# Piece products as 128 + 64 rows, two steps' half-height products in a row, and a new end of the routed sum, in a two-layer ViT tower

## The chip, the cores and the metric

The kernel runs on one core of a Trainium2 chip. The metric is the device time of one execution in microseconds (us), lower is better. All times below are those of one core.

## The reference, cut to what matters

Activations are 1,024 tokens (64 images of 16 patches) by 192 features, in float32. After the patch embedding come four residual blocks, each behind a layer norm:

```python
h = tok(x)
h = h + attn0(layernorm(h))                 # 12 heads over the 16 patches of an image
h = h + ffn0(layernorm(h))                  # soft mixture: 4 experts x 256 slots
h = h + attn1(layernorm(h))                 # low-rank causal attention
h = h + ffn1(layernorm(h))                  # routed mixture: 4 of 32 experts for a token
# ffn0
logits = einsum('bnd,esd->bnes', x, phi)    # 1024 logits for a token
dispatch = softmax(logits, axis=1)          # over the 16 tokens of an image
combine = softmax(logits.reshape(B, N, E*S))
slots = einsum('bnd,bnes->besd', x, dispatch)
hid = gelu(einsum('besd,edh->besh', slots, w1) + b1)
y = einsum('besh,ehd->besd', hid, w2) + b2
out = einsum('besd,bnes->bnd', y, combine)
# ffn1: comb holds 4 non-zero gates for each token
h = gelu(einsum('nd,edm->nem', xf, W1) + b1)
out = einsum('ne,ned->nd', comb, einsum('nem,emd->ned', h, W2) + b2)
```

## The kernel before

Tokens stand in 8 tiles of 128. The stages follow each other, each in a block of its own in which every engine has its own instruction list, with counted semaphores between them. SP's list issues nearly all DMAs, POOL's the indirect ones; a wait in a list holds everything behind it.

**layernorm** (L150) is called ahead of each of the four blocks. DVE normalises a tile (L188), PE transposes it in two pieces of 96 features (L199), ACT copies the pieces to `xnT` (96 partitions, two chunks, 1,024 tokens; L211).

**slot_weights** (L729). For each tile PE computes 1,024 logits: two halves of 512 columns, each the sum of two products of 96 rows (L770 to L773). PE also transposes logits and weights (L764), ACT copies and exponentiates, DVE takes maxima and sums. PE's order is logits 0, logits 1, then for each tile transposes of the logits, transposes of the weights of the tile before, logits of the tile two on.

**hidden_pieces** (L876) computes x·w1 for all tokens (3,072 columns) and writes it, and the transposed dispatch weights, to DRAM (`pieces`) as three bf16 pieces that add up to the float32 value. There are 8 tiles of 5 steps. Step 0 is 8 transposes (L934). Steps 1 to 4 are one expert each: two halves of 384 columns, each the sum of two float32 products of 96 rows (L939). A float32 product is two matmul instructions in the trace, so such a step has 8 instructions. A step's result lies in one of 4 PSUM buffers (`gps`). ACT makes the first piece ("one", L961), DVE subtracts it into `rest` (L984, semaphore `rest1`), ACT makes the second piece ("two", L955), DVE the third by another subtraction (L978, semaphore `three`). ACT's order is one(n), second(n-1); DVE's is rest(n), third(n-1). PE may start step n when `rest1` says that step n-4 has left its buffer (L931). The pieces of a tile stand in one of two SBUF buffers (`gp`); from tile 2 on ACT waits until the stores of the tile two before have landed (L960). SP stores a tile in three DMAs (L903): after step 0, after step 2, after step 4. Behind the stores of tile 2 SP's list has the loads of the first two images for the next stage (L912 to L918): 3 small ones and 12 of `load_image`.

**slot_experts** (L990) runs the 64 images in sequence and is the longest stage. Its PE needs the two images and all earlier work of the block before.

**expert_tiles** (L1425) runs the routed experts: 63 tiles of 128 rows, 3 buffers deep, 9 tiles in a loop body. PE transposes gathered rows (L1496), then computes the 6 hidden chunks as full-height products of 128 rows and half-height products of 64 rows, the latter in two row groups in turn (L1508, L1511), and the result of the tile before (L1523). DVE scales it into `y` (L1598) and POOL adds it by an indirect DMA to the rows of one of three sums in DRAM (`sums`: the output and two others; L1644), one sum for each buffer. In the last round the last three tiles all go to the output, each waiting for the one before. POOL adds the third sum to the second (L1661) once both are complete, and, after the last tile, the second to the output (L1669). Each of these is a DMA with addition in DRAM (L1649). The kernel ends when the last has landed.

Of the kernel before, what the change touches and what calls it, by code (L numbers as in the profile page):

```python
# [15 lines left out]
P = 128  # L16
# [25 lines left out]
KQ = 64  # L42
# [107 lines left out]
def layernorm(nc, g, stage, banks=None, loads=(), loaded=None):  # L150
# [4 lines left out]
    with Scope(nc, stage) as s:  # L155
# [5 lines left out]
            s.sem(n) for n in ("stats_ready", "mv_ready", "step", "var_ready", "sd_ready", "xn_ready", "t_ready", "xnT_done"))  # L161
        block = s.block()

# [6 lines left out]
        def _(dve):  # L170
# [16 lines left out]
            for i in range(TILES):  # L187
                dve.tensor_scalar(g.xn[:, i, :], g.h[:, i, :], r[:, i:i + 1], nmr[:, i:i + 1],  # L188
                                  ALU.mult, ALU.add).then_inc(xn_ready, 1)

        @block.tensor
        def _(pe):
            pe.wait_ge(g.ident_in, 16)
            keep_busy(pe, g, psT[-1], 16)
            for i in range(TILES):
                pe.wait_ge(xn_ready, i + 1)
                for k in range(NKD):
                    at = (i % 2 * NKD + k) * P
                    tr = pe.transpose(psT[i // 2][0:KD, at:at + P], g.xn[:, i, k * KD:(k + 1) * KD], g.ident[:])  # L199
                tr.then_inc(t_ready, 1)  # L200

        @block.scalar
        def _(act):
            act.wait_ge(var_ready, 1)
            act.activation(sd[:], ve[:], ACT.Sqrt).then_inc(sd_ready, 1)
            for j in range(TILES // 2):
                act.wait_ge(t_ready, 2 * j + 2)
                for k in range(NKD):
                    src = psT[j][0:KD, :].rearrange("p (i k c) -> p i k c", i=2, k=NKD)[:, :, k, :]
                    dst = g.xnT[:, k, 2 * j * P:(2 * j + 2) * P].rearrange("p (i c) -> p i c", i=2)  # L210
                    act.activation(dst, src, ACT.Copy).then_inc(xnT_done, 1)  # L211
# [517 lines left out]
def slot_weights(nc, g, CT, Dn, zn):  # L729

    with Scope(nc, "slw") as s:
# [26 lines left out]
        def _(pe):  # L759
# [7 lines left out]
            def logits(i):  # L767
                if i >= 2:
                    pe.wait_ge(lg_ready, i - 1)
                for half in range(2):  # L770
                    for k in range(NKD):
                        mm = pe.matmul(cl[:, i % 2, half, :], g.xnT[:, k, i * P:(i + 1) * P],
                                       g.phi[:, k, half * 512:(half + 1) * 512], start=(k == 0), stop=(k == NKD - 1))  # L773
# [102 lines left out]
def hidden_pieces(nc, g, Dn, b1, b2_rows, pieces, b_dram):  # L876
# [3 lines left out]
    with Scope(nc, "hid") as s:  # L880
        gp = s.sb("gp", [P, 2, 3, ALL], BF16)
        rest = s.sb("rest", [P, 2, ALL_SLOTS])
# [3 lines left out]
        b_in, step, g_ready, one, rest1, two, three, b_done, g_out = (  # L886
            s.sem(n) for n in ("b_in", "step", "g_ready", "one", "rest1", "two", "three", "b_done", "g_out"))
# [4 lines left out]

        def half_of(e):
            return 512 if e == 0 else HALF

        @block.sync
        def _(sp):
# [7 lines left out]
            for i in range(TILES):  # L905
                sp.wait_ge(three, STEPS * i + 1)
                store(i, slice(WIDE, ALL))
                for half in range(2):
                    sp.wait_ge(three, STEPS * i + 2 * half + 3)
# [11 lines left out]
        def _(pool):  # L921
            for i, dT in enumerate(g.dT):
                pool.memset(dT[PROWS:BROWS, :], 1.0).then_inc(g.ones, 1)
                pool.wait_ge(g.ones, i + 1)

        @block.tensor
        def _(pe):
            pe.wait_ge(g.w1_in, 16)
            for n, (i, e) in enumerate(steps):
                if n >= 4:  # L930
                    pe.wait_ge(rest1, n - 3)  # L931
                if e == 0:
                    for c in range(SLOT_CHUNKS):
                        mm = pe.transpose(gps[n % 4][:, c // 4, (c % 4) * P:(c % 4 + 1) * P], Dn[:, c, i * P:(i + 1) * P], g.ident[:])  # L934
                else:
                    for half in range(2):
                        for k in range(NKD):
                            at = (e - 1) * HID + half * HALF
                            mm = pe.matmul(gps[n % 4][:, half, 0:HALF], g.xnT[:, k, i * P:(i + 1) * P],  # L939
                                           g.w1[:, k, at:at + HALF], start=(k == 0), stop=(k == NKD - 1))  # L940
                mm.then_inc(g_ready, 1)

        def piece(buf, k, e):
            at = slice(WIDE, ALL) if e == 0 else slice((e - 1) * HID, e * HID)
            return gp[:, buf, k, at].rearrange("p (a c) -> p a c", a=2)

        def left(n, e):
            return rest[:, n % 2, 0:2 * half_of(e)].rearrange("p (a c) -> p a c", a=2)
# [872 lines left out]
```

## Time and profile before

| | |
|---|---|
| three runs | 1148.75, 1153.36, 1153.44 us; median 1153.36 |
| the profiled execution | 1146.11 us, of which the span from its first to its last instruction is 1144.3 us |
| mean granted clock of TensorE in it | 0.946 of full speed |
| PE, matmuls | 1015.9 us busy (89%) |
| ACT | 671.7 us (59%) |
| DVE | 403.2 us (35%) |
| POOL | 232.7 us (20%) |

The stages in the profiled execution, by the times at which they start: attention 0 and what is ahead of it 0 us, the layer norm 84, slot_weights 89, hidden_pieces 148, slot_experts 246, attention 1 about 690, routing about 775, expert_tiles 823 to 1144.3.

How to read it: the profiled execution's time is 1.8 us above its span, and lies 7.2 us under the median of the three runs. Busy time of PE is modelled at the end of each matmul, so a group of matmuls shows slightly longer than the distance to the next group. A clock of 1.0 is 2.4 GHz, one of 0.5 is 1.2 GHz.

### The profile page before, as it was taken

What the parts mean: (1) busy time and instruction counts of PE and PEld (TensorE: products, weight loads), DVE (VectorE), ACT (ScalarE), POOL (GpSimd) and SP (SyncE); (2) the same over time, 40 slices, a digit from 0 to 9 for tenths busy, and PEclk for the clock granted to TensorE, in tenths of its full rate; (3) what the DMA queues carried; (4) which work ended last, traced back from release to release, by engine and by line L of the source; (5) the groups of instructions that cost most, each with busy time, mean ns of one, the idle gap of its engine ahead of it and who ended that gap; (6) DMA issues with size and microseconds to landing.
All of it is one profiled execution on the core that took longest, in us unless ns stands there. A gap on an engine that the chain in (4) does not pass through costs nothing. (4 is left out here: it accounts for less than half of the span.)

```text
span 1144.3 us, 22007 instructions
## 1 busy us (share of the span) xinstructions
PE 1015.9 (89%) x7432; PEld 668.2 (58%) x7432; DVE 403.2 (35%) x1027; ACT 671.7 (59%) x1227; POOL 232.7 (20%) x236
## 2 busy tenths in 40 slices
PE   8879689989999999999999998873299999999992
PEld 7455456633444444444445454452189999999992
DVE  2666968750111111111111115767822222222220
ACT  0657957679988888888788852451033433343330
POOL 0110310000000000000000000200655555555532
PEclk9999889989999999999999998896589999999997
DMA  9200037979555445455444401004199999999994
GB/s 278 79 2 0 1 125 262 340 270 172 120 117 134 111 114 127 95 124 124 112 111 117 106 1 46 0 6 129 49 326 313 311 307 306 309 309 307 304 288 73
DMA packets 72411, 183.74 MB, mean 161 GB/s; under 512 B 15712, under 2 KB 30400, under 8 KB 72008
## 3 DMA queue, kind: packets, MB, share of 16 engines
q1 hardware_dynamic: 59260, 166.24, 48.7%
q0 software_dynamic: 12640, 16.16, 7.1%
q8 instruction: 53, 0.87, 0.3%
q10 hardware_dynamic: 432, 0.26, 0.1%
q14 instruction: 26, 0.21, 0.1%
HBM read 147.52 MB, written 36.67 MB: 161 GB/s over the span
## 5 line engine op out<-in xcount | busy, mean ns | idle before, releaser
L1145 ACT ACTIVATE sle_H<-sle_hp 128x1024 f32<-128x1024 f32 x384 | 367.5, 1024 | 61.1 <-PE sle_hp L1082 61.1
L1565 ACT ACTIVATE ext_H<-ext_hp,ext_bias 128x128 f32<-128x128 f32 x378 | 104.3, 375 | 171.9 <-issue 153.8
L1099 PE MATMUL sle_up<-sle_H,sle_cw 128*32 128x512 f32 (+1 forms) x2048 | 193.5, 496 | 0.0
L1523 PE MATMUL ext_yp<-ext_w,ext_H 128*128 128x192 f32 x756 | 139.7, 335 | 2.2 <-ACT ext_H L1565 1.6
L1160 DVE STREAM_TRANSPOSE sle_UT<-sle_up 128x256 f32<-128x256 f32 x64 | 37.3, 583 | 295.1 <-PE sle_up L1099 295.1
L1523 PEld LDWEIGHTS ext_yp<-ext_w,ext_H 128*128 128x128 f32 x756 | 121.1, 190 | 10.0 <-issue 2.6
L1082 PE MATMUL sle_hp<-keep_G,keep_dT 99*128 99x512 bf16 (+1 forms) x512 | 103.6, 337 | 10.9 <-PEq L880 5.7
L1099 PEld LDWEIGHTS sle_up<-sle_H,sle_cw 128*32 128x32 f32 x2048 | 53.8, 109 | 87.6 <-issue 74.2
L1082 PE MATMUL sle_hp<-sle_G,sle_dT 99*128 99x512 bf16 (+1 forms) x512 | 99.9, 327 | 1.1 <-ACT sle_H L1145 1.1
L1067 POOL COPY sle_cw<-keep_CT 128x128 f32 (+1 forms) x64 | 18.7, 293 | 396.1 <-PE sle_up L1099 396.0
L1508 PE MATMUL ext_hp<-ext_xT,ext_w 128*128 128x128 f32 x756 | 96.1, 277 | 0.0
L1082 PEld LDWEIGHTS sle_hp<-keep_G,keep_dT 99*128 99x128 bf16 x512 | 45.6, 100 | 82.4 <-issue 30.0
L1508 PEld LDWEIGHTS ext_hp<-ext_xT,ext_w 128*128 128x128 f32 x756 | 90.6, 194 | 0.3 <-DMA ext_w<-W 0.3
L939 PE MATMUL hid_gps<-pre_w,vit_xnT 96*128 96x384 f32 x256 | 85.7, 494 | 0.0
L1082 PEld LDWEIGHTS sle_hp<-sle_G,sle_dT 99*128 99x128 bf16 x512 | 44.4, 98 | 69.4 <-ACT sle_H L1145 30.3
L1576 DVE COPY ext_yi<-rmoe_slot 128x1 uint32 (+1 forms) x63 | 9.7, 154 | 208.1 <-PE ext_yp L1523 172.9
L1644 POOL DMA_INDIRECT sum<-ext_y,ext_yi x40 | 63.4, 1584 | 71.0 <-DVE ext_gate L1589 32.7
L939 PEld LDWEIGHTS hid_gps<-pre_w,vit_xnT 96*128 96x128 f32 x256 | 49.0, 194 | 32.8 <-issue 1.7
L1108 PE MATMUL sle_up<-keep_w,sle_UT 128*128 128x192 f32 x384 | 67.3, 326 | 0.8 <-DVE sle_UT L1160 0.8
L1631 POOL DMA_INDIRECT ext_x<-xn,ext_xi x63 | 62.1, 985 | 27.3 <-issue 18.6
L1108 PEld LDWEIGHTS sle_up<-keep_w,sle_UT 128*128 128x128 f32 x384 | 61.7, 190 | 2.1 <-DVE sle_UT L1160 1.7
L1511 PE MATMUL ext_hp<-ext_xT,ext_w 64*128 64x128 f32 x756 | 59.7, 291 | 0.0
(258 smaller groups left out, 1158.2 us busy)
## 6 DMA issues: line engine op xcount, KB each, us to landing
ext_w<-W SPq DMA_DIRECT2D x126, 576.0 KB
pieces<-hid_gp SPq DMA_DIRECT2D x16, 1152.0 KB, 4.9
keep_G<-pieces SPq DMA_DIRECT2D x32, 288.0 KB, 3.9
sle_G<-pieces SPq DMA_DIRECT2D x32, 288.0 KB, 3.8
pieces<-hid_gp SPq DMA_DIRECT2D x8, 768.0 KB, 4.7
keep_G<-pieces SPq DMA_DIRECT2D x32, 192.0 KB, 3.8
sle_G<-pieces SPq DMA_DIRECT2D x32, 192.0 KB, 3.7
keep_CT<-xT SPq DMA_DIRECT2D x6, 512.0 KB, 6.2
```

The lines of the kernel that those rows point to most:

```text
L939: mm = pe.matmul(gps[n % 4][:, half, 0:HALF], g.xnT[:, k, i * P:(i + 1) * P], g.w1[:, k, at:at + HALF], start=(k == 0), stop=(k == NKD - 1))
L1082: mm = pe.matmul(hp[k % DEEP][:, j, off:off + width], dT[b][:, c * P:(c + 1) * P], G[b][:, (c // 2) * HID + at:(c // 2) * HID + at + width ...
L1099: mm = pe.matmul(to[32 * e:32 * e + 32], cw[:, p, 2 * e + grp, :], H[:, p, h:h + width], start=(p == 0 and grp == 0), stop=(p == 1 and grp ...
L1108: mm = pe.matmul(yps, UT[:, par, b, :], g.w2[:, b, :], start=(b == blocks[0]), stop=(b == blocks[-1]))
L1145: act.activation(H[:, p, WIDTH * k:WIDTH * (k + 1)], hp[k % DEEP][:].rearrange("p a c -> p (a c)"), ACT.Gelu_apprx_tanh).then_inc(gelu_don ...
L1160: dve.transpose(UT[:, par, at // 32:(at + width) // 32, 32 * j:32 * j + 32], src.rearrange("p (b c) -> p b c", c=32)).then_inc(ut_done[ban ...
L1508: pe.matmul(hp[q][:, c % 2, (c // 2) * P:(c // 2 + 1) * P], w1[:, q, c, :], xT[:, q, 0, :], start=(c < 2), stop=False)
L1511: mm = pe.matmul(hp[q][:, c % 2, (c // 2) * P:(c // 2 + 1) * P], w1[rows, q, HC + c // 2, :], xT[rows, q, 1, :], start=False, stop=(c >= H ...
L1523: mm = pe.matmul(yp[:, 0:D], H[:, q, c, :], w2[:, q, c, :], start=(c == 0), stop=(c == HC - 1))
L1565: act.activation(H[:, q, c, :], hp[q][:, c % 2, (c // 2) * P:(c // 2 + 1) * P], ACT.Gelu, bias=bias[:, q, c:c + 1]).then_inc(gelu_done, 1)
L1631: pool.indirect_dma_start(out=x[:, p, :], out_offset=None, in_=xn_dram, in_offset=bass.IndirectOffsetOnAxis(ap=xi[p][:], axis=0)).then_inc ...
L1644: pool.indirect_dma_start(out=sums[to], out_offset=bass.IndirectOffsetOnAxis(ap=yi[q][:], axis=0), in_=y[:, q, :], in_offset=None, compute ...
```

## The change

Four edits:

1. `layernorm` has a form `wide`, used ahead of `slot_weights`: POOL copies features 128 to 191 of each tile once more behind feature 191 (`xn` has 256 columns now), and PE transposes two full chunks of 128. Rows 0 to 127 of the first chunk are features 0 to 127; of the second, rows 0 to 63 and rows 64 to 127 both are features 128 to 191. `phi` and `w1` are laid out to match on the host, with the same number of bytes.
2. In `slot_weights` each half's logits are a product of 128 rows and one of 64 rows; the two halves' 64-row products use different row groups and stand behind each other.
3. `hidden_pieces` does the same, over two steps (experts) at a time: first the four full-height products of both, then their four half-height ones. `rest` has three buffers instead of two. The third pieces of steps 2 and 4 are made by POOL instead of DVE, with semaphores `three_dve` and `three_pool` for those who wait.
4. In `expert_tiles` the last two tiles are not scattered. DVE makes 0/1 matrices `place` from their row numbers, PE multiplies them with `y` (8 token tiles x 2), SP loads the three sums to SBUF, DVE adds them and the products in PSUM, and SP stores the result to the output in two halves. The two additions in DRAM are gone.

```diff
 def layernorm(...):
+        if wide:
+            @block.gpsimd
+            def _(pool):
+                for i in range(TILES):
+                    pool.wait_ge(xn_ready, i + 1)
+                    pool.tensor_copy(g.xn[:, i, D:D + KQ], g.xn[:, i, P:D]).then_inc(twice_ready, 1)
...
+                if wide:
+                    pe.wait_ge(twice_ready, i + 1)
+                    for k in range(NKD):
+                        tr = pe.transpose(psT[i // 2][:, at + k * P:at + (k + 1) * P], g.xn[:, i, k * P:(k + 1) * P], g.ident[:])
 def slot_weights(...):
                 for half in range(2):
-                    for k in range(NKD):
-                        mm = pe.matmul(cl[:, i % 2, half, :], g.xnT[:, k, i * P:(i + 1) * P],
-                                       g.phi[:, k, half * 512:(half + 1) * 512], start=(k == 0), stop=(k == NKD - 1))
+                    pe.matmul(cl[:, i % 2, half, :], g.wideT[:, 0, i * P:(i + 1) * P], g.phi[:, half * 512:(half + 1) * 512],
+                              start=True, stop=False)
+                for half in range(2):
+                    rows = slice(half * KQ, (half + 1) * KQ)
+                    mm = pe.matmul(cl[:, i % 2, half, :], g.wideT[rows, 1, i * P:(i + 1) * P], g.phi[rows, ALL_SLOTS:],
+                                   start=False, stop=True)
 def hidden_pieces(...):
-        rest = s.sb("rest", [P, 2, ALL_SLOTS])
+        rest = s.sb("rest", [P, 3, ALL_SLOTS])
+        ON_POOL = (2, 4)
...
         def _(pool):
+            for n, (i, e) in enumerate(steps):
+                if e in ON_POOL:
+                    pool.wait_ge(two, n + 1)
+                    pool.tensor_tensor(piece(i % 2, 2, e), left(n, e), piece(i % 2, 1, e), ALU.subtract).then_inc(three_pool, 1)
 
         @block.tensor
+            def free(n):
                 if n >= 4:
                     pe.wait_ge(rest1, n - 3)
...
+                for pair in range(1, STEPS, 2):
+                    for e in (pair, pair + 1):
+                        free(STEPS * i + e)
+                        for half in range(2):
+                            pe.matmul(gps[(STEPS * i + e) % 4][:, half, 0:HALF], g.wideT[:, 0, tokens],
+                                      g.w1[:, e - 1, half * HALF:(half + 1) * HALF], start=True, stop=False)
+                    for e in (pair, pair + 1):
+                        for half in range(2):
+                            rows = slice(half * KQ, (half + 1) * KQ)
+                            mm = pe.matmul(gps[(STEPS * i + e) % 4][:, half, 0:HALF], g.wideT[rows, 1, tokens], g.w1[rows, e - 1, HID:],
+                                           start=False, stop=True)
+                        mm.then_inc(g_ready, 1)
         @block.vector
-                if n >= 2:
-                    dve.wait_ge(three, n - 1)
+                if n >= 3:
+                    wait_thirds(dve, *steps[n - 3])
                 dve.tensor_tensor(left(n, e), gps[n % 4][:, :, 0:half_of(e)], piece(i % 2, 0, e), ALU.subtract).then_inc(rest1, 1)
-                if n >= 1:
+                if n >= 1 and steps[n - 1][1] not in ON_POOL:
                     third(n - 1)
 def expert_tiles(...):
         @block.sync
             program(sp, load)
+            sp.wait_ge(y_out[1], 16 * (MOE_TILES // DEEP - 1))
+            sp.dma_start(second[:], by_lane(sums[1])).then_inc(second_in, 16)
+            sp.wait_ge(first_out, 32)
+            sp.wait_ge(y_out[0], 16 * (MOE_TILES // DEEP))
+            sp.dma_start(g.h[:], by_lane(out)).then_inc(first_in, 16)
+            sp.wait_ge(y_out[2], 16 * (MOE_TILES // DEEP - 1))
+            sp.dma_start(third[:], by_lane(sums[2])).then_inc(third_in, 16)
+            for j in range(2):
+                half = slice(j * TILES // 2, (j + 1) * TILES // 2)
+                sp.wait_ge(whole, 2 * j + 2)
+                sp.dma_start(by_lane(out)[:, half], second[:, half]).then_inc(total_out, 16)
         @block.tensor
             down(MOE_TILES - 1, BODY - 1, ROUNDS - 1)
+            pe.wait_ge(place_ready, PLACED)
+            pe.wait_ge(y_done, MOE_TILES)
+            for i in range(TILES):
+                for n in range(PLACED):
+                    mm = pe.matmul(hp[i // 4][:, i % 4 // 2, i % 2 * D:(i % 2 + 1) * D], place[:, n, i, :], y[:, (n - PLACED) % DEEP, :],
+                                   start=(n == 0), stop=(n == PLACED - 1))
+                if i % 2 == 1:
+                    mm.then_inc(placed, 1)
         @block.vector
+            def total():
+                dve.wait_ge(second_in, 16)
+                dve.wait_ge(first_in, 16)
+                c.after(dve.tensor_tensor(second[:], second[:], g.h[:], ALU.add))
+                dve.wait_ge(third_in, 16)
+                c.after(dve.tensor_tensor(second[:], second[:], third[:], ALU.add))
+                for j in range(4):
+                    pair = second[:, 2 * j:2 * j + 2]
+                    dve.wait_ge(placed, j + 1)
+                    dve.tensor_tensor(pair, pair, hp[j // 2][:, j % 2, 0:2 * D].rearrange("p (a d) -> p a d", a=2), ALU.add).then_inc(whole, 1)
         @block.gpsimd
-            merge(0, 1)
-            pool.wait_ge(merged, 32)
+            pool.wait_ge(y_out[0], 16 * (MOE_TILES // DEEP))
```

Besides, SP loads two small constants (68 KB) behind the first store of the output in `expert_tiles`, and DVE makes the two `place` matrices in the last round, at tiles 55 and 57.

## Rows read from the trace of the kernel before

**Rows 1.** Busy time by stage: us, PE, PEld, DVE, ACT, POOL, clock, DMA share, GB/s

```profile
89.00:148.00 59.00, 45.27 (x194) 27.40 (x195) 45.56 (x64) 48.53 (x98) 15.74 (x9) 0.90 0.00 1
148.00:241.00 93.00, 92.17 (x320) 56.60 (x319) 74.94 (x81) 63.16 (x79) 1.60 (x2) 0.97 0.72 266
```

**Rows 2.** Timeline of PE in hidden_pieces: start us, us, engine, line, operation

```profile
147.75 1.94 PE L934 MATMUL hid_gps<-vit_ident,pre_Dn 128*128 128x128 f32 x8 [3.21 <-PEq L732]
...
184.02 1.04 PE L934 MATMUL hid_gps<-vit_ident,pre_Dn 128*128 128x128 f32 x8
184.89 10.49 PE L939 MATMUL hid_gps<-pre_w,vit_xnT 96*128 96x384 f32 x32
195.22 1.04 PE L934 MATMUL hid_gps<-vit_ident,pre_Dn 128*128 128x128 f32 x8
```

**Rows 3.** The chain that ended last, one routed tile: start us, us, what

```profile
1103.40 1.34 PE ext_hp L1508 x12
1104.74 0.87 PE ext_hp L1511 x12
1105.61 2.15 PE ext_yp L1523 x12
```

**Rows 4.** Timeline at the end of hidden_pieces, ACT, DVE and PE

```profile
240.21 0.81 ACT L961 ACTIVATE hid_gp<-hid_gps 128x768 bf16<-128x768 f32 x1 [0.70 <-PE hid_gps L939]
...
242.40 1.95 DVE L978 TENSOR_TENSOR hid_gp<-hid_rest,hid_gp 128x768 bf16<-128x768 f32 x2
...
245.87 4.42 PE L1082 MATMUL sle_hp<-keep_G,keep_dT 99*128 99x512 bf16 x13 [5.70 <-PEq L880]
```

**Rows 5.** Groups of instructions, each shape apart, POOL: busy us, mean ns

```profile
L860 POOL TENSOR_TENSOR pre_Dn<-pre_Dn,slw_dsum 128x1024 f32<-128x1024 f32 x8 | 15.4, 1931 | 51.3 <-DVE slw_dsum L832 51.3
L1067 POOL COPY sle_cw<-keep_CT 128x128 f32<-128x128 f32 x16 | 4.6, 292 | 83.1 <-PE sle_up L1099 83.0
```

**Rows 6.** Timeline in routing, POOL and DVE side by side

```profile
806.15 1.46 POOL L1288 TENSOR_TENSOR rte_row_in<-rte_in_tile,rte_row_lane 128x504 bf16<-128x504 f32 x1
806.65 2.05 DVE L1404 TENSOR_TENSOR rte_in_lane<-rte_lane,rte_lanef 128x1024 bf16<-128x1024 f32 x1
```

**Rows 7.** Timeline of SP's DMA issues and of ACT in hidden_pieces

```profile
189.10 0.53 SPq L903 DMA_DIRECT2D pieces<-hid_gp  x1
...
201.01 2.60 SPq L903 DMA_DIRECT2D pieces<-hid_gp  x2
...
211.54 1.02 ACT L961 ACTIVATE hid_gp<-hid_gps 128x1024 bf16<-128x1024 f32 x1 [3.38 <-DMA pieces<-hid_gp]
```

**Rows 8.** Busy time of three short stretches, columns as in rows 1

```profile
203.00:205.00 2.00, 2.00 (x8) 1.20 (x7) 1.51 (x3) 0.97 (x2) 0.00 (x0) 1.00 1.05 404
250.00:252.00 2.00, 2.00 (x8) 0.97 (x7) 0.00 (x0) 2.00 (x3) 1.88 (x4) 0.50 0.19 57
1129.00:1131.00 2.00, 0.00 (x0) 0.00 (x0) 0.00 (x0) 0.00 (x0) 1.50 (x1) 0.59 0.00 0
```

**Rows 9.** Timeline at the start of slot_weights, DVE

```profile
97.55 1.22 DVE L842 TENSOR_REDUCE slw_dmax<-slw_dl 128x64 f32<-128x1024 f32 x1 [2.03 <-PE slw_dl L764]
```

**Rows 10.** Timeline of the end of the kernel

```profile
1118.21 1.55 POOL L1644 DMA_INDIRECT out<-ext_y,ext_yi  x1 [3.05 <-DVE ext_y L1598]
...
1124.44 0.41 DVE L1598 TENSOR_SCALAR ext_y<-ext_yp,ext_gate 128x192 f32<-128x192 f32 x1
...
1133.00 0.96 POOL L1649 DMA_DIRECT2D out<-sum  x1 [2.50 <-DMA out<-ext_y,ext_yi]
```

**Rows 11.** The chain that ended last, its DMAs at the end

```profile
1122.85 5.21 DMA out<-ext_y,ext_yi
1128.93 3.52 DMA out<-ext_y,ext_yi
```

**Rows 12.** DMA issues by line: count, KB each, median us from issue to landing

```profile
pieces<-hid_gp SPq DMA_DIRECT2D x16, 1152.0 KB, 4.9
xn<-vit_xn SPq DMA_DIRECT2D x1, 768.0 KB, 4.2
out<-sum POOLq DMA_DIRECT2D x1, 768.0 KB, 7.0
```

More of the change, by code:

```diff
@@ L147, in _, with layernorm @@
             dve.wait_ge(h_done, TILES)
-def layernorm(nc, g, stage, banks=None, loads=(), loaded=None):
+def layernorm(nc, g, stage, banks=None, loads=(), loaded=None, wide=False):
     with Scope(nc, stage) as s:
@@ L928, in _ @@
             pe.wait_ge(g.w1_in, 16)
-            for n, (i, e) in enumerate(steps):
+            def free(n):
                 if n >= 4:
                     pe.wait_ge(rest1, n - 3)
[L932 to L948, printed above, removed]
+            for i in range(TILES):
+                tokens = slice(i * P, (i + 1) * P)
+                free(STEPS * i)
+                for c in range(SLOT_CHUNKS):
+                    tr = pe.transpose(gps[STEPS * i % 4][:, c // 4, (c % 4) * P:(c % 4 + 1) * P], Dn[:, c, tokens], g.ident[:])
+                tr.then_inc(g_ready, 1)
+                for pair in range(1, STEPS, 2):
[10 more added lines that the diff above has]
+                        mm.then_inc(g_ready, 1)
         @block.scalar
@@ L1442, in expert_tiles @@
         shareT = s.sb("shareT", [P, 2, P])
+        lane, steps = s.sb("lane", [P, P]), s.sb("steps", [P, TILES])
+        rowf, first_row, place = s.sb("rowf", [P, PLACED]), s.sb("first_row", [P, PLACED, TILES]), s.sb("place", [P, PLACED, TILES, P])
+        second, third = (s.sb(n, [P, TILES, D]) for n in ("second", "third"))
         xi = [s.sb(f"xi{i}", [P, 1], U32) for i in range(BODY)]
@@ L1624, in _ @@
             leave_y(MOE_TILES - 1, BODY - 1, ROUNDS - 1, False)
+            total()
         @block.gpsimd
@@ L1655, in tile @@
                     gather(t + BODY, p)
-                if not (first and p == 0):
-                    scatter(t - 1, (p - 1) % BODY, r + (p - 1) // BODY, first and p <= DEEP, last and p > 0)
-                if last and p == BODY - DEEP + 1:
-                    for q in range(1, DEEP):
-                        pool.wait_ge(y_out[q], 16 * (MOE_TILES // DEEP - 1))
-                    merge(1, 2)
+                if not (first and p == 0) and not (last and p > BODY - PLACED):
+                    scatter(t - 1, (p - 1) % BODY, r + (p - 1) // BODY, first and p <= DEEP)
             for q in range(BODY):
```

95 lines of the change are left out of this document (60 added, 35 removed).

## The prediction

> **What bounds the kernel now.** I read the busy time by stage first. In hidden_pieces PE is busy 92.2 of 93 us, DVE 74.9, ACT 63.2 [rows 1]. The timeline of PE gives its period: 11.20 us from one tile's transposes to the next's, of which 0.87 is the 8 transposes and 10.33 the 32 instructions of L939, 0.323 us each [rows 2]. So this stage follows PE. In slot_weights PE is busy 45 of 59 us and ACT 48.5 [rows 1]; ACT stands still there almost only at the start. Last the end: the final result leaves DVE at 1124.85 and the span ends at 1144.3, 19.4 us in which only scatters and the last addition in DRAM run [rows 10, 11].
>
> **Full and half height.** The routed tiles show the price of both forms: 12 full-height instructions of 128 columns take 1.34 us (0.112 each), 12 half-height ones in alternating row groups 0.87 [rows 3]. That fits "each starts with the second instruction of the one before": 12 half-height ones then need 7 slots, 0.78 us, and 0.09 is left for going in and out. Rows (96 or 128) don't change a full-height slot, columns do.
>
> **hidden_pieces, PE.** Two steps were 16 slots of 0.323. Now they are 8 full-height slots (2.58 us) and 8 half-height instructions in 5 slots plus 0.09 (1.70 us): 4.28 us. A tile takes 0.87 + 2 x 4.28 = 9.43 us, 1.77 less. Ends of the price: no overlap, 11.2 us a tile; halves for nothing, 6.0. I take the slots, as the nearest row has the same form. The Trainium skill ("TensorEngine Tiling (Array Packing)", Key Properties) says that a change of tiling mode drains TensorE. If each of the four changes in a tile cost the 0.16 us by which a matmul of L939 outlasts its slot (below), a tile would take 9.9 us instead of 9.4, and the eight save some 10 us instead of 14.
>
> DVE now needs 74.9/8 = 9.4 us a tile. Two subtractions of 0.95 us leave it [rows 4], which makes 7.5. ACT stays at 7.9. On POOL 1,024 elements with two inputs took 1.93 us, 768 are 1.45, twice a tile [rows 5]. All are under 9.43, so PE keeps the stage, and eight tiles would save 14.1 us.
>
> **What is late next: the stores of tile 3.** SP issued the last store of tile 2 at 189.10, 5.1 us after PE left that tile for the transposes of tile 3 (184.02), then 15 loads, and the last store of tile 3 only at 201.01. ACT could write tile 5 at 211.54, after 3.4 us of waiting [rows 2, 7]: 21.9 us after SP entered the loads (about 189.65). PE didn't notice: step 4 of tile 5 waits for the subtraction of step 0, which was done at 211.54 + 1.02 + 1.22 = 213.8, and PE came there at 206.41 + 0.87 + 3 x 2.58 = 215.0. This reserve of 1.2 us is gone in the new kernel. With P for the time at which PE leaves tile 2:
> - the last third is ready at P + 5.5: one(3) can start at P - 0.64 (two slots before the end), then second(2), one(4), second(3), 0.71 us each, end at 2.2; one(0) of the next tile ends at 3.15, second(4) at 4.0, and POOL takes 1.5. SP enters the loads at P + 6.15.
> - DMA was at full share (404 GB/s) here [rows 8], and SP's issues take what they took, so the 21.9 us stay: tile 5 may be written from P + 28.0, and its step 0 has left PSUM at P + 30.4.
> - PE wants to start step 4 of tile 5 at P + 18.86 + 0.87 + 4.28 + 1.29 = P + 25.3. It **stands for 5.1 us**.
>
> And it restarts cold. After PE's 5.7 us of idle time at 240.17 [rows 4] the granted clock was still 0.50 at 250 to 252 [rows 8], 6 us after the restart; at the end of the kernel it fell about 5 us after PE stopped (0.59 in 1129 to 1131) [rows 8]. [...] I take 6 us at half speed, 3.0 us lost; nothing or 3.0 are the ends.
>
> Stage before: 147.75 to 240.17, 92.4 us. Now: tile 0 13.87 - 1.77 = 12.1 (13.87 is 184.02 - 2 x 11.20 - 147.75), two tiles 18.9, to the end of tile 5 33.4 (30.4 + 1.29 + 1.70), clock 3.0, two tiles 18.9: 86.2. **Gain 6.2.**
>
> The handing over gets longer. Before, the last third was done at 244.35, 4.2 us after PE [rows 4]. Now ACT has two steps to finish (one(4) to P + 1.6, rest to 2.6, second to 3.5) and POOL takes 1.5: P + 5.1. **Cost 0.9.** The third `rest` buffer and the new waits cost nothing while POOL's 1.5 us fit in the two steps until its buffer is wanted.
>
> **Layer norm and logits.** POOL's copy stands between DVE and PE once (then it keeps pace: at most 0.29 us for 64 columns [rows 5] against a tile each 0.30): 0 to 0.6, I take 0.4 cost. Logits of a tile were 8 slots of 0.43 us (0.323 x 512/384), now 4 + 3 and 0.09: 0.34 less. Two of them stand ahead of the first maximum, for which DVE waited 2.03 us [rows 9]: 0.7 gained. Later ones are hidden by ACT; without that cover they would give up to 2 us more. **Gain 0.3.** xn's longer rows in the other layer norms, and phi and w1 of the same size and loaded long before, cost nothing.
>
> **The end.** Tile 60's scatter starts at 1118.21 and lands like the last one did, undisturbed, after 3.52 us [rows 10, 11]: 1121.7. SP then issues the load of the output sum. 768 KB in the same rows of 768 bytes took 4.2 us the other way, the DRAM addition 7.0 [rows 12]; these are my ends, and I take 4.2: 1126.0, and 2.4 for the third sum behind it: 1128.4 (the second sum is loaded long before). DVE adds 1,536 elements in 1.83 us (1.22 x 1.5 [rows 9]): 1130.3. PE's 32 instructions of 192 columns at 0.179 [rows 3] run from 1125 to 1130.7, beside this. Four adds of 384 (0.46 each) end at 1132.2, the second store of 384 KB lands 3.5 later (between 2.5 and 4.2): 1135.7. Before, the last addition was issued at 1133.0 and landed at 1140.0; 4.3 us followed, which I keep: 1140.0 against 1144.3. **Gain 4.3**, between 6 and -1 by the ends. SP's two loads of constants go out after its long issue at the first tiles, where it then waits for PE. The `place` matrices (1.2 us each) fall on a DVE that waits for PE most of each tile, right behind the scaling of y, and the next copy it owes PE is wanted a good part of a tile later: nothing.
>
> **Sum.** 6.2 - 0.9 + 0.3 + 4.3 = 9.9 us. The profiled execution's 1146.1 becomes 1136.2, its span 1134.4. That execution lies 7.2 us below the median of the three runs; against the median, 1153.4, the forecast is **1143.5 us**. A measurement here tells about 0.5% (5.8 us) from no change.
>
> **Rivals.**
> - *No stall in tile 5* (stores land earlier, or the clock stays up and only the pause remains). The pause rests on one measured distance of 21.9 us; for it speaks that SP's list is unchanged. Without it the gain is 14.1 - 0.9 + 0.3 + 4.3 = 17.8: 1135.6. Chance 0.20.
> - *DVE and POOL block each other.* In routing, a DVE comparison with two SBUF inputs took 2.05 us, of which 0.96 lay beside one of POOL's and 1.09 behind its end, as if it had waited [rows 6]. If each POOL third holds up a DVE third, DVE needs 7.5 + 3.0 = 10.5 us a tile and becomes the bound; eight tiles then save 5.6, no stall of PE follows, and with the rest the gain is 5.6 - 0.9 + 4.6 = 9.3 less some 3 for waits in the chain of tile 5: 6, 1147.4. Against it: POOL starts its third when DVE is at a subtraction from PSUM, which has one SBUF input. Chance 0.08. The Trainium skill ("SBUF — State Buffer", Who interferes with whom) says that a DVE instruction with two SBUF inputs contends with a GpSimd one that reads SBUF, one with a single SBUF input does not; rows 6 agree with the first half.
> - *The end gives nothing.* If the loads take 7 us as the additions did, the first sum is there at 1128.7, the third about 1132, the end about 1144.5. The gain is 5.4: 1148. Chance 0.12.
> - *Slower.* The half-height products of 384 columns don't run beside each other but each waits until the one before has left the array. A matmul of L939 lasts about 0.16 us beyond its slot (10.49 busy against 10.33 to the next group [rows 2]). 16 such a tile cost 2.6 us on top of the old 11.2; eight tiles lose 21, the end gives 4 back: 1170. It decides from a mean half-height slot of 0.35 us on (break-even of the whole change); rows 3 show 0.65 of a full slot. Chance 0.07.
> - The forecast's own case: 0.53.
>
> **Numbers.** Faster by over 0.5%: nearly all of the first case (0.48), all of no stall (0.20), half of the blocking and a third of the end case (0.08): 0.76. Slower: 0.07 and 0.01 for a dearer end. Same: 0.16. The range goes from the no-stall case less the runs' own spread, 1131, to the small-gain cases plus some, 1151.
>
> **What would show it.** L939's successors: full-height 0.323 and half-height about 0.21 us a piece, tile period 9.4. A gap of PE of about 5 us before step 4 of tile 5, ACT's wait for the stores of tile 3 at some 10 us, and a clock of 0.50 behind the gap. DVE's thirds at 0.95 us and POOL's at 1.5. The gap between hidden_pieces and slot_experts at 6.6 instead of 5.7 us. At the end, the two loads at 4 to 5 us, the span ending about 15 us after the last y instead of 19.4. Wrong would be: no gap (then 1136), a tile period over 10 (packing or DVE), or a gap in other tiles as well, from the chain landing, one(0), second(4), POOL, store (4.9 us), which I put at 9.6 us, just above the period.

## The result, and the profile after the change

Four runs of the changed kernel took 1136.42 to 1137.72 us, median 1136.94; beside them the kernel before had a median of 1151.05. The ratio is 0.9887, 95% interval 0.9845 to 0.9928: faster by about 13 us. A second set of seven runs (the last experiment) gave 0.9895 [0.9845, 0.9941]. The forecast was 1143.5 us, in a range of 1131 to 1151, and a gain of 9.9 us.

The profiled execution took 1137.21 us, its span 1135.4 us, at a mean clock of 0.945. Its busy times, from the page:

```profile
span 1135.4 us, 22122 instructions
PE 1011.5 (89%) x7464; PEld 659.8 (58%) x7464; DVE 396.8 (35%) x1021; ACT 669.8 (59%) x1227; POOL 256.9 (23%) x256
```

Busy time hardly moved: PE lost 4.4 us of 1,016. What the kernel gained lies in the order of things, so the places have to be read one by one. **hidden_pieces**, by line, in the stretch from its first transposes to 241 us, just behind PE's last instruction (DVE's and POOL's last ones lie behind it; busy us, mean ns of one, idle time before and its releaser; answers to [rows 1, 2]):

```profile
L979 PE MATMUL hid_gps<-pre_w,vit_xnT 128*128 128x384 f32 x128 | 48.0, 520 | 5.4 <-DVE hid_rest L1022 5.4
L1022 DVE TENSOR_TENSOR hid_rest<-hid_gps,hid_gp 128x768 f32<-128x768 f32 (+1 forms) x39 | 39.4, 1010 | 23.1 <-ACT hid_gp L999 23.1
L984 PE MATMUL hid_gps<-pre_w,vit_xnT 64*128 64x384 f32 x128 | 26.1, 528 | 0.0
L960 POOL TENSOR_TENSOR hid_gp<-hid_rest,hid_gp 128x768 bf16<-128x768 f32 x14 | 23.0, 1644 | 57.0 <-ACT hid_gp L993 57.0
```

The timeline of PE, one tile early in the stage, and the place where PE stood:

```profile
162.45 2.85 PE L979 MATMUL hid_gps<-pre_w,vit_xnT 128*128 128x384 f32 x8
165.23 1.56 PE L984 MATMUL hid_gps<-pre_w,vit_xnT 64*128 64x384 f32 x8
166.72 1.10 PE L973 MATMUL hid_gps<-vit_ident,pre_Dn 128*128 128x128 f32 x8
167.66 2.75 PE L979 MATMUL hid_gps<-pre_w,vit_xnT 128*128 128x384 f32 x8
170.33 1.56 PE L984 MATMUL hid_gps<-pre_w,vit_xnT 64*128 64x384 f32 x8
...
209.28 1.56 PE L979 MATMUL hid_gps<-pre_w,vit_xnT 128*128 128x384 f32 x4
216.24 2.93 PE L979 MATMUL hid_gps<-pre_w,vit_xnT 128*128 128x384 f32 x4 [5.40 <-DVE hid_rest L1022]
219.10 2.67 PE L984 MATMUL hid_gps<-pre_w,vit_xnT 64*128 64x384 f32 x8
```

Starts of groups are the measure, since their ends are modelled: eight full-height instructions take 2.67 or 2.78 us, eight half-height ones 1.49, the transposes 0.93; a tile 9.37 us. At 216.24 stands the forecast pause, 5.40 us long, and behind it the same eight half-height instructions take 2.60 us. ACT at the same place, and the clock there (columns as in [rows 1]):

```profile
213.90 1.02 ACT L999 ACTIVATE hid_gp<-hid_gps 128x1024 bf16<-128x1024 f32 x1 [7.27 <-DMA pieces<-hid_gp]
```

```profile
216.00:219.00 3.00, 2.76 (x4) 1.18 (x4) 2.79 (x4) 2.73 (x4) 1.37 (x1) 0.50 0.59 239
219.00:222.00 3.00, 3.00 (x12) 1.49 (x12) 1.65 (x3) 1.20 (x2) 0.00 (x0) 0.60 1.03 413
222.00:225.00 3.00, 3.00 (x16) 1.97 (x14) 2.53 (x4) 3.00 (x5) 1.65 (x1) 1.00 0.50 193
```

The end of the stage (answers to [rows 4]):

```profile
244.09 1.64 POOL L960 TENSOR_TENSOR hid_gp<-hid_rest,hid_gp 128x768 bf16<-128x768 f32 x1 [0.93 <-ACT hid_gp L993]
...
247.29 1.01 PE L1119 MATMUL sle_hp<-keep_G,keep_dT 99*128 99x512 bf16 x3 [6.79 <-PEq L897]
```

And the **end of the kernel**, from its timeline (answers to [rows 10, 11]):

```profile
1117.40 1.55 POOL L1729 DMA_INDIRECT out<-ext_y,ext_yi  x1 [3.05 <-POOLq L1728]
...
1120.94 0.39 SPq L1537 DMA_DIRECT2D vit_h<-out  x1
...
1121.39 0.57 SPq L1539 DMA_DIRECT2D ext_third<-sum  x1
...
1123.36 0.41 DVE L1663 TENSOR_SCALAR ext_y<-ext_yp,ext_gate 128x192 f32<-128x192 f32 x1
...
1125.91 1.76 DVE L1688 TENSOR_TENSOR ext_second<-ext_second,vit_h 128x1536 f32<-128x1536 f32 x1 [2.14 <-DMA vit_h<-out]
1128.26 1.76 DVE L1690 TENSOR_TENSOR ext_second<-ext_second,ext_third 128x1536 f32<-128x1536 f32 x1 [0.60 <-DMA ext_third<-sum]
1130.06 1.95 DVE L1694 TENSOR_TENSOR ext_second<-ext_second,ext_hp 128x384 f32<-128x384 f32 x4
1131.10 1.31 SPq L1543 DMA_DIRECT2D out<-ext_second  x2
```

From the end of the last y to the end of the span it was 19.45 us and is now 11.63.

**Where the time went**, read from the timelines of the two profiled executions and of the changed kernel's second one (the last experiment). All in us:

| | before | after | after, second |
|---|---|---|---|
| layer norm ahead of slot_weights starts at | 85.5 | 93.3 | 85.5 |
| from there to hidden_pieces | 62.3 | 61.6 | 61.6 |
| hidden_pieces, PE's first to last instruction | 92.4 | 85.6 | 83.8 |
| idle time to slot_experts | 5.70 | 6.79 | 6.79 |
| slot_experts to the last y | 879.0 | 876.5 | 880.1 |
| last y to the end of the span | 19.45 | 11.63 | 11.57 |
| span | 1144.3 | 1135.4 | 1129.4 |

The first row is a trap. The two profiled executions differ by 8.9 us, but the second one entered the layer norm 7.8 us late, in code that both kernels share. Of these, 2.1 us were there already at the first product of attention 0's scores, with the granted clock at 1.00 in both (the kernel before, then the kernel after):

```profile
40.57 0.53 PE L394 MATMUL at_b<-pre_Dn,at_qT 98*32 98x192 f32 x8 [0.28 <-DVE at_qT L497]
```

```profile
42.70 0.53 PE L408 MATMUL at_b<-pre_Dn,at_qT 98*32 98x192 f32 x8 [0.28 <-DVE at_qT L511]
```

They come from the embedding, where PE's 96 products start at 6.81 instead of 5.95 us and take 17.22 instead of 15.98. The other 5.7 us arise while TensorE's granted clock is low (attention 0 of the kernel after, then of the kernel before, columns as in [rows 1]):

```profile
48.00:51.00 3.00, 3.00 (x7) 1.57 (x6) 0.36 (x1) 0.88 (x2) 0.00 (x0) 0.50 0.00 0
51.00:54.00 3.00, 3.00 (x5) 0.97 (x4) 1.58 (x3) 0.00 (x0) 0.00 (x0) 0.50 0.00 0
...
69.00:72.00 3.00, 3.00 (x32) 1.54 (x35) 1.47 (x3) 0.00 (x0) 0.00 (x0) 0.50 0.02 5
```

```profile
48.00:51.00 3.00, 3.00 (x8) 0.98 (x6) 3.00 (x5) 1.42 (x3) 0.00 (x0) 1.00 0.00 0
51.00:54.00 3.00, 1.94 (x5) 0.57 (x4) 1.27 (x2) 3.00 (x6) 0.00 (x0) 1.00 0.00 0
...
69.00:72.00 3.00, 2.41 (x57) 1.70 (x59) 2.76 (x7) 2.85 (x7) 0.77 (x2) 1.00 0.02 5
```

The second execution of the changed kernel has its first score product at 40.56 us, has the clock at 1.00 there and starts the layer norm at 85.5. The 14 profiled executions of this document divide the same way: in five the first score product stands at 40.56 to 40.97 us, the clock stays at 1.00 from 40 to 78 us, and the layer norm starts at 85.5 to 86.3; in nine it stands at 41.09 to 42.70, the clock falls to 0.50 behind it, and the layer norm starts at 88.6 to 93.5. That the late start brings the fall isn't shown.

The clock also makes most of the difference between the 85.6 us of hidden_pieces in one execution of the changed kernel and the 83.8 in the other. The stage begins at a low clock in all of them. Its first tile, tile 0, took 13.88 us before, and 11.81 and 10.66 after, with a mean clock over the stage's first 10 us of 0.73, 0.75 and 0.86. Tile 5, the one with the pause, took 17.52 and 16.86. All other tiles take the same in both, 9.37 us (the last 9.43).

Compared with the second execution, the change is worth 14.9 us by the profile, of which about 1.2 are the clock in that first tile; the ratio of the runs says some 13.

### The profile page after: what moved, and what is told of

It reads as the page before. It is cut to its first block and busy times, and to the rows that moved or that the text cites. A ratio compares the mean times of both kernels' runs of the same rounds, so it can differ in the third digit from the quotient of the medians.

```text
span 1135.4 us, 22122 instructions
## 1 busy us (share of the span) xinstructions
PE 1011.5 (89%) x7464; PEld 659.8 (58%) x7464; DVE 396.8 (35%) x1021; ACT 669.8 (59%) x1227; POOL 256.9 (23%) x256
## 5 line engine op out<-in xcount | busy, mean ns | idle before, releaser
L979 PE MATMUL hid_gps<-pre_w,vit_xnT 128*128 128x384 f32 x128 | 48.0, 520 | 5.4 <-DVE hid_rest L1022 5.4
L1568 PEld LDWEIGHTS ext_hp<-ext_xT,ext_w 64*128 64x128 f32 x756 | 47.1, 187 | 7.6
```

The source lines that it names most:

```text
L979: pe.matmul(gps[(STEPS * i + e) % 4][:, half, 0:HALF], g.wideT[:, 0, tokens], g.w1[:, e - 1, half * HALF:(half + 1) * HALF], start=True, s ...
L1568: mm = pe.matmul(hp[q][:, c % 2, (c // 2) * P:(c // 2 + 1) * P], w1[rows, q, HC + c // 2, :], xT[rows, q, 1, :], start=False, stop=(c >= H ...
```

## The experiments

Five questions were open: whether the forecast's parts are the right ones (both ends of the kernel apart), whether the loads make the pause, whether two steps in a row pay, what a half-height product really does, and where 3.5 us at the end came from that no term of the forecast held. Ratios are to the kernel before, run on the same chip beside each; its own median was 1148.19, 1149.03 and 1151.61 us in the three sets, so the medians of different sets can't be held against each other.

**The end alone, and all but the end.** The first is the kernel before with only the fourth edit, the second the changed kernel with the scatters and DRAM additions of before at its end.

> The kernel before with edit 4 alone (new end). 11.6 us from the last y to the end; about 8 us faster than the kernel before, 1143. hidden_pieces as before: 92.4 us, no pause of PE. Together with the run on the old end it tells whether the two parts add up to the whole gain of 13 us: 7.8 for the end would leave some 5 to 6 for hidden_pieces and what is around it.

> Edits 1 to 3 with the end of the kernel before (three scatters in a row, two additions in DRAM). The end in the traces was 19.4 us from the last y to the end of the span before and 11.6 after, 7.8 us less, where 4.3 were forecast. If that holds, this kernel ends 19.4 us after its last y and is 7.8 us slower than the changed one, about 1145. Rival (chance of one execution): the end takes 16 us or less here.

End alone: 1140.78 us median of 12, ratio 0.9943 [0.9916, 0.997]; hidden_pieces 92.5 us, from the last y to the end 11.76. All but the end: 1144.43 of 12, ratio 0.9942 [0.9907, 0.9978]; hidden_pieces 84.3 with a pause of 5.3, the end 19.67. By the ratios each is worth 6.6 us (give or take 3 and 4), both together 13: they add within that, and in the timelines neither touches the other's stage. By the timelines the stages are worth 92.4 + 5.7 - 85.6 - 6.8 + 0.7 = 6.4 and the end 7.8.

**The loads spread.** Instead of both images behind tile 2, SP issues one of the six runs of load_image behind each tile from 2 to 7.

```diff
-                    for n in range(2):
-                        load_image(sp, pieces, n, g.G[n], g.dT[n], g.image_in[n])
+                if i >= 2:
+                    n, k = (i - 2) // 3, (i - 2) % 3
+                    load_run(sp, pieces, n, g.G[n], g.dT[n], g.image_in[n], k)
```

> The new kernel with the 12 image loads of tile 2 spread out: two behind the stores of each of tiles 2 to 7 (the three small loads stay at tile 2). Theory (SP's 10 us of load issues hold back tile 3's stores, ACT waits 7.3 us at tile 5, PE stands 5.4 us and restarts at half clock): no pause of PE over 1 us in hidden_pieces, no low clock behind it, the stage 85.5 - 5.4 - about 2.8 = 77.3 us from its first transpose to PE's end, the kernel some 8 us faster than the changed one, about 1129 us. Rival (the stores themselves are the bound, DMA at full share): the pause moves to another tile or splits up, and the stage keeps 83 us or more.

1127.86 us median of 6, ratio 0.9853 [0.9803, 0.9903]. PE has no gap, and the stage takes 76.3 us, 7.5 or 9.3 less than in the changed kernel's two executions (7.5 is the fair figure: the first tile takes 10.65 us here and 10.66 in that one). But the last loads now stand behind the last stores in SP's list, and the idle time grows to 8.85:

```profile
229.34 1.05 SPq L887 DMA_DIRECT2D keep_dT<-pieces  x1
230.44 1.15 SPq L889 DMA_DIRECT2D keep_G<-pieces  x1
...
232.31 4.00 PE L1131 MATMUL sle_hp<-keep_G,keep_dT 99*128 99x512 bf16 x12 [8.85 <-PEq L908]
```

So SP's loads made the pause, as the forecast had it. Stage and handover together take 85.15 us instead of 90.6 or 92.4, so 5.4 us are kept with like first tiles. The whole kernel was expected to be 8 us faster than the changed one; by the ratios it is some 4 us, and the two intervals overlap, so this gain rests on the timelines.

**The same loads spread in the kernel before**, as a control.

> The kernel before the change, with its fifteen loads spread over the tiles as in the spread version of the changed one. Theory (before, the stores of tile 3 cost PE nothing, so the loads' place pays only together with the shorter tiles): hidden_pieces stays at 92.4 us within 0.5, the idle time before slot_experts grows by 0 to 3 us as it did with the changed kernel, and the whole is not faster than before. Rival (the loads slow the stage in another way, as by contention of DMA): the stage gets shorter by more than 1 us here too.

The twelve image loads were spread; the three small ones stay at tile 2. 1152.6 us median of 10, ratio 1.0007 [0.9968, 1.0045]; hidden_pieces 92.5, idle 6.66. Before the change the reserve of PE covered the loads; their place costs only together with the shorter tile.

**Loads spread over tiles 2 to 6, and the very last third on DVE.**

```diff
+        def on_pool(i, e):
+            return e in ON_POOL and not (i == TILES - 1 and e == STEPS - 1)
...
+                for n, k in {2: [(0, 0)], 3: [(0, 1)], 4: [(0, 2)], 5: [(1, 0)], 6: [(1, 1), (1, 2)]}.get(i, ()):
```

> The changed kernel with its loads spread over tiles 2 to 6, and the very last third of hidden_pieces on DVE instead of POOL. If SP's fifteen loads in a row made the pause and POOL's third (1.64 us, with its waits) sets the handover: no gap of PE, hidden_pieces at 76 to 77 us, the idle time before slot_experts 6 to 7 us instead of 8.85, and the kernel 1.5 to 3 us faster than with the loads spread alone. If the handover is set by loads that now land last instead, it stays at 8 to 9 us.

1128.57 us median of 6, ratio 0.9824 [0.978, 0.9867]; the idle time is 6.01 us, hidden_pieces 78.0, the two together 84.0 against 85.15. The handover went as expected; the stage is 1.0 us over the expected 76 to 77. All of its 1.7 us over the other spread version lie in the first tile (12.34 us against 10.65, at a mean clock of 0.70 against 0.87 in the stage's first 10 us); the other tiles take the same. The medians of the two spread versions can't be told apart; in the timelines this one's stage and handover are 6.6 to 8.4 us shorter than the changed kernel's. Both are clear of the kernel before; their intervals overlap with the changed kernel's. I would keep the second.

**One step at a time.** The half-height products of a step directly behind its own full-height ones, with the loads as in the changed kernel and then with the loads spread.

```diff
-                for pair in range(1, STEPS, 2):
-                    for e in (pair, pair + 1):
+                for pair in range(1, STEPS):
+                    for e in (pair,):
```

> The new kernel, but each step's two half-height products right behind its own two full-height ones, not two steps' in a row. By slots a step is 4 x 0.323 + 3 x 0.323 + 0.09 = 2.35 us and a tile 0.87 + 4 x 2.35 = 10.3 us instead of 9.36. Theory (the time to the end of tile 5 is set by the stores of tile 3, not by PE): PE's pause shrinks from 5.4 us to under 1.5, the low clock behind it goes, and the stage takes about 85.5 us as now, so the kernel is the same within 2 us. Rival (PE's own time sets the stage): 8 x 0.9 = 7 us slower than the changed kernel.

> The same spread loads, but every step's two half-height products directly behind its own full-height ones (four changes of height more a tile). Theory (putting two steps in a row saves slots once nothing else sets the time): 4 half-height products take 3 slots instead of 2.5, a tile of 9.9 to 10.3 us instead of 9.36, hidden_pieces at 80 to 84 us instead of 76.3. Rival (the order is worth nothing): 76 to 77 us.

With the changed kernel's loads: 1131.32 us median, ratio 0.9868 [0.9825, 0.991], hidden_pieces 85.2 (pause 2.22, where under 1.5 was expected), idle 6.0. Here the order by pairs brings nothing that these runs can tell: the stores of tile 3 set the time, and a slower PE only waits less. With the loads spread: 1139.1 us median of 6, ratio 0.9871 [0.9821, 0.9921], hidden_pieces 82.9 and idle 7.43, together 4.2 to 5.2 us more than with two steps in a row (86.1 in the kernel after the next one and 85.15 in the first spread version). The timeline gives its period, from one row of transposes to the next:

```profile
166.81 1.10 PE L985 MATMUL hid_gps<-vit_ident,pre_Dn 128*128 128x128 f32 x8
...
169.13 0.92 PE L996 MATMUL hid_gps<-pre_w,vit_xnT 64*128 64x384 f32 x4
169.97 1.56 PE L991 MATMUL hid_gps<-pre_w,vit_xnT 128*128 128x384 f32 x4
...
176.98 1.09 PE L985 MATMUL hid_gps<-vit_ident,pre_Dn 128*128 128x128 f32 x8
```

10.17 us with eight changes of height a tile, 9.37 with four. Take transposes of 0.87, 16 full-height instructions of 0.323 and 16 half-height ones of half that, 8.62 together: the rest is 0.75 for four changes and 1.55 for eight, **0.19 us a change both times**, as a mean of going in and coming out. With that the half-height products themselves cost half a slot, and not the 0.62 to 0.75 that the forecast and this theory took.

**All half-height products in one row group.** Only the upper 64 rows are used; the features of the lower rows are left out of the second half.

```diff
-                            mm = pe.matmul(..., g.wideT[rows, 1, tokens], g.w1[rows, e - 1, HID:],
+                            mm = pe.matmul(..., g.wideT[0:KQ, 1, tokens], g.w1[0:KQ, e - 1, HID:],
```

> Spread loads; every half-height product takes the upper 64 rows of its operands, so no product of the lower ones stands in the kernel's widest products (the 32 last features of the reduction and their copies are taken twice from the upper rows and not from the lower ones). Theory (two half-height products overlap because they lie in different row groups): all eight need the same rows, take a full slot of 0.33 each, 2.7 us instead of 1.49, and hidden_pieces takes 16 x 1.2 = 19 us longer, about 96. Rival (a half-height product costs about half a slot by itself, whichever rows it uses): 1.49 us and 76 to 77 us.

```profile
169.72 2.75 PE L991 MATMUL hid_gps<-pre_w,vit_xnT 128*128 128x384 f32 x8
172.39 2.84 PE L996 MATMUL hid_gps<-pre_w,vit_xnT 64*128 64x384 f32 x8
175.17 2.85 PE L991 MATMUL hid_gps<-pre_w,vit_xnT 128*128 128x384 f32 x8
```

Eight take 2.78 us instead of 1.49, hidden_pieces 98.0 us, the kernel 1151.16 (ratio 0.9976 [0.9932, 1.002]). The saving is overlap between row groups and nothing else. The tile of 11.94 us is 0.87 + 32 x 0.323 and 0.73 for its four changes of height, 0.18 each: the same price without any halves to assume. Without the overlap the stage is slower than before the change, and the new end and the spread loads only make up for that.

**The same row group twice running.** The two products of the upper rows, then the two of the lower.

> Spread loads; of the eight half-height products of two steps, the first step's and the second step's product of the same row group stand next to each other, so only every second product changes the row group. Theory (two half-height products overlap only where neighbours lie in different row groups): 8 take 6 slots of 0.33 or more, about 2.0 us instead of 1.49, a tile about 10.4 us, hidden_pieces about 84. Rival (a half-height product is simply cheaper, whatever stands beside it): 1.49 us and 76 us as before.

1131.12 us median of 4, ratio 0.9813 [0.9759, 0.9867], hidden_pieces 77.0, and eight still take 1.5 us. My theory was wrong here. The single matmul records of one block (start us, length in ns; the order of the code is upper four, lower four) show pairs that start within 14 ns, four pairs 0.32 us apart:

```
160.816 587    161.243 482    161.565 483    161.888 482
160.830 587    161.256 482    161.579 482    161.901 482
```

The second record of the second pair (161.256) and that of the fourth (161.901) are the ones that signal a finished step. In the code these are the sixth and the last of the eight, so the sixth, of the lower rows, started ahead of the third and the fourth, of the upper rows. The row groups run side by side over the whole block, so neighbours needn't alternate.

**All thirds on DVE**, with spread loads.

> The changed kernel with spread loads and all five thirds of a tile on DVE, none on POOL. DVE's work is then 5 x (subtraction from PSUM + third), about 9.3 us a tile against PE's 9.36. Theory (POOL's two thirds are needed only barely): hidden_pieces 76.3 to 80 us, with idle moments of PE of below 1 us, and 6 instead of 8.85 us before slot_experts. Rival (DVE's waits come on top and it becomes the bound): over 82 us.

1131.89 us median of 4, ratio 0.9843 [0.9778, 0.9909], hidden_pieces 77.9 (first tile 12.23), idle 8.31 where 6 was expected, no gap of PE. DVE stands idle for 1.6 us of 68, and yet PE's period doesn't grow. POOL's share of the thirds brings the stage nothing that these runs can tell. The idle time answers a question of the version with loads up to tile 6, which changed two things at once: with the last third on DVE and the loads up to tile 7 it is still 8.31 us and not 6.01, so it is the place of the last loads, more than the engine of the last third, that sets the handover there. SP's last load is issued at 235.05 us, the next stage's PE starts at 236.38.

**The final stores on POOL's queue.** The changed kernel, but POOL issues the two stores of the sum.

> The changed kernel with the two stores of the final sum issued by POOL instead of SP. Theory (what the end gained beyond the forecast is POOL's own draining of its queue, 3.9 us after its last transfer landed before the change): the time from the last y to the end of the span becomes 11.6 + 3.5 to 4.5 = 15 to 16 us. Rival (the gain came from elsewhere, as cheaper transfers): 11.6 to 12.5 us.

1141.92 us median of 9, ratio 0.993 [0.9898, 0.9962]; from the last y to the end 16.90 us, 0.9 over the expected range and far from the rival's. The largest part is an instruction that the profile doesn't count as busy. The trace's sequencer records hold a DRAIN of POOL (start us, length us):

```
before                    1140.15  3.906
all but the end           1140.67  3.906
end alone                 1121.52  3.579
after                     1121.06  3.579
final stores on POOL      1138.02  3.742
```

It stands at the end of POOL's list, behind its wait for the landing of its last transfer. Where POOL issues the kernel's last DMA, it is the last thing in the span (1140.15 + 3.91 = 1144.06 of 1144.3), so the kernel before doesn't end with the landing of its last addition, as I had written of it, but with this; where SP does, it ends 11 us ahead of the end. Moving two stores cost 16.90 - 11.63 = 5.3 us, of which 3.7 are this. Of the rest, 0.8 us is a slower landing of the second store (3.73 us after its issue instead of 2.95) and some 0.5 its later issue, since POOL's issue of the first takes 0.85 us.

**The changed kernel again**, unaltered.

> The changed kernel once more, unaltered. Theory (the granted clock in attention 0, the same code in both kernels, falls to 0.50 in some executions and not in others, and is worth about 7 us): the median within 1136 to 1141, single runs spread over 1129 to 1141 in two groups, and the profiled execution has layer norm 1 at 85.5 or at 93.3 us and the end of the span 51 us or 43 us less than 1187 accordingly: 1128 or 1135.4. Rival (layer norm 1 starts late because of the change): 93.3 us again and no run under 1133.

1137.92 us median of 7 (1131.23 to 1140.35). The profiled execution starts the layer norm at 85.5 and has a span of 1129.4, a pause of 5.25 and the same idle time of 6.79. The late start isn't the change's. The kernel before with spread loads shows the same from the other side: there the clock stood at 0.50 from 46 to 50 us, and the layer norm started at 89.0. Two clear groups of runs didn't show.

## Why the prediction was right, and where a number was off

**PE's tile: right total, wrong split.** Forecast 9.43 us, measured 9.37. The forecast took 10 slots for 16 half-height instructions and 0.09 for each block's entry and exit. The runs show 8 slots and 0.19 for each change of height: two errors that cancel, since both make 0.8 us a tile over the bare 8.6. The rule of the Trainium skill ("TensorEngine Tiling (Array Packing)", Key Properties) that a change of mode drains TensorE was rated too low: the trace agrees with it, at 0.19 us a change. The 9.9 us that I worked out from it failed only because it put the drain on top of two slots that don't exist.

**The pause: right.** Forecast 5.1 us before step 4 of tile 5, from the stores of tile 3; measured 5.40, 5.25, 5.3 and 5.44 in four executions of the three kernels with that code and those loads. PE left tile 2 at 185.46; tile 5 was written 28.4 us later (forecast 28.0), and PE wanted step 4 25.4 us later (25.3). ACT waited 7.27 us where I had some 10. The clock: 5.46 us for twelve instructions that take 2.8 warm, so 2.6 lost (forecast 3.0).

**The stage:** gain 6.8 and 8.6 us in two executions, forecast 6.2. The 6.8 belongs to the execution whose clock at the stage's start was like the one before (0.75 and 0.73); in the other, 1.2 us are the first tile's clock, which the forecast didn't look at. The no-stall rival was a true alternative and is what the spread loads make: stage and handover together are 98.1 before and 85.15 there, a gain of 12.95 where it held 13.2 (14.1 less 0.9). That this fits so well is luck: the stage gained 16.1, with the first tile's clock and eight times 1.83 instead of 1.77 us in it, and the handover cost 3.15.

**Handover:** 6.79 for 5.70, cost 1.1; forecast 0.9. POOL's third takes 1.64 us, not 1.45.

**Layer norm and logits:** forecast gain 0.3; 62.3 became 61.6, a gain of 0.7.

**The end is the term that was mis-sized: forecast 4.3, measured 7.8.** Up to the last store its steps held. The scatter landed after 3.47 us (3.52); the load of the output sum took 5.0 (4.2), the third sum was there 0.6 us later than forecast, DVE's first additions took 1.76 each (1.83), and DVE ended 14.6 us after the issue of tile 60's scatter (1117.4 to 1132.0), 14.0 by the forecast (1118.2 to 1132.2). The failed step is the sentence "4.3 us followed, which I keep". I took what followed the last landing for a fixed cost of the end of a kernel. 3.9 of it was POOL's drain, which the new end hides: the span ends 3.4 us after DVE's last addition, no more than the 3.5 that I had for the store alone (it landed 2.95 us after its issue). From the last y to the end I had 15.15 us, and it was 11.63. The drain and the quicker store make 4.4 of this; the slower loads, and a last y that stood 0.3 us nearer to tile 60's scatter, took back 0.9.

**The sum:** 9.9 forecast; 14.9 between executions with the same start. Of the 5.0 missing the end makes 3.6, the stage 2.4 (half of it the clock of its first tile) and the logits 0.4; the longer handover and the unchanged stages take 1.3 back. By the ratios the gain is some 13. The measured 1136.9 lies nearer to the 1135.6 of the no-stall rival than to the forecast's 1143.5, but not for that rival's reason: the pause came. Another 2.3 us of the distance are that the kernel before itself ran at 1151.05 beside these runs and not at 1153.4. The result lay within the range because the other terms were near.

**The rivals.** Blocking between DVE and POOL didn't come: DVE's 768-element subtractions take 0.95 us as before, and the argument (one input of DVE's lies in PSUM when POOL works) held. The end gave more, not nothing. The slower case is what the one-row-group kernel measured. A half-height product cost 0.35 us there (2.78 for eight), the point that the forecast named as break-even for the whole change, and with the better end and the spread loads besides that kernel is just even with before. Its price was mis-sized: a tile is 11.94 us, 0.7 over the old 11.20 and not 2.6, because a product waits for the slot of the one before and not for its whole way through the array.

Still open: why attention 0's clock falls in some executions and not in others, and whether the later start of its first score product in those executions brings it about. The layer norm's and the logits' part was read from timelines and not run by itself.

## What to carry to other kernels

When a stage's engine gets faster, write down for each buffer when it is wanted and when its store lands: a reserve of 1.2 us turned into a pause of 5.4 here, and moving twelve loads in SP's list gave back 5.4 us in the timelines, almost as much as the rewritten products had brought net of that pause (6.4). Ask of the last microseconds of a span which engine's they are, before calling them fixed. And before comparing two profiled executions, compare the time at which they enter the first changed stage, and the granted clock at which they begin it.

## What the hardware showed that I had not expected

- A DRAIN of POOL of 3.6 to 3.9 us stands behind the landing of its last DMA in expert_tiles, in all five kernels looked at. It cost nothing where SP issued the kernel's last transfer, and 3.7 to 3.9 us at the end of the span where POOL did.
- Half-height float32 products of two row groups run fully side by side (starts 14 ns apart), also where four of one group stand in the code ahead of four of the other. A change between full and half height costs 0.19 us on average, by the tile periods of three kernels (9.37, 10.17 and 11.94 us).
- The granted clock falls to 0.50 in an unchanged stage in nine of 14 profiled executions, and the next stage then starts 3 to 8 us late, up to 2.1 of them from before the fall; the 23 runs of the kernel before beside the last experiments spread over 1142.76 to 1159.05 us.
